# Attention over a long context: probabilities transposed on VectorE and moved by SBUF transfers instead of on TensorE, blocks handled in pairs

## The reference

```python
Q_char = _linear(layernorm(x), Wq_c, bq_c)                 # 256 x 512
K_sub  = _linear(ctx, Wk_s, bk_s)                          # 25088 x 512
V_sub  = _linear(ctx, Wv_s, bv_s)
scores = einsum('bqh,bkh->bqk', Q_char, K_sub) / sqrt(512)
char2sub = einsum('bqk,bkh->bqh', softmax(scores), V_sub)
...
x = x + gate * char2sub + (1 - gate) * sub2char            # sub2char: the other direction, on sampled rows
x = x + attention(layernorm(x)); x = x + moe(layernorm(x))
```

## Time and profile before

| | us |
|---|---|
| median of 3 runs (lowest, highest) | 1259.25 (1258.22, 1261.04) |
| profiled execution, its own time | 1258.86 |
| its span, first to last instruction | 1257.0 |
| prologue, to the first matmul of the block loop | 78.6 |
| block loop, to the last addition of `acc` | 654.0 |
| one block in the loop | 11.77 |
| busy in the span: PE, DVE, ACT | 1117.1, 578.9, 392.4 |

### The profile page before, as it was taken

The page is one execution under the profiler, slowest core; times in us unless marked ns, Lnnn a source line. Parts: engine busy times, 40 slices in busy tenths (PEclk is TensorE's granted clock), DMA queues, the critical chain, the costliest instruction groups (busy, mean ns, idle before and its releaser), DMA issues.

```text
span 1257.0 us, 17677 instructions
## 1 busy us (share of the span) xinstructions
PE 1117.1 (89%) x7048; PEld 785.6 (62%) x7048; DVE 578.9 (46%) x955; ACT 392.4 (31%) x645; POOL 3.5 (0%) x20
## 2 busy tenths in 40 slices
PE   9999999999999999999999989998876656665767
PEld 8768888888888888888887657655322222222223
DVE  2367777777777777777743165220110010001001
ACT  1254554554554554554522163101100000000000
POOL 1000000000000000000000000000000000000000
PEclk9999999999999999999999989999998998989988
DMA  9158455455455455455508315997999999999996
GB/s 361 69 224 331 153 194 188 154 192 190 153 191 191 151 191 192 151 190 193 174 1 351 118 67 202 373 380 290 422 418 421 421 425 421 422 422 421 423 419 283
DMA packets 84780, 331.07 MB, mean 263 GB/s; under 512 B 3600, under 2 KB 3728, under 8 KB 75408
## 3 DMA queue, kind: packets, MB, share of 16 engines
q1 hardware_dynamic: 84752, 330.66, 67.7%
HBM read 330.12 MB, written 0.52 MB: 263 GB/s over the span
## 4 chain that ended last, share of the span: by engine, by line
PE 71%; SPq 23%; DMA 3%; DVE 2%; issue 1%; ACT 1%; DVEq 0%
SPq L372 17%; PE ps L507 7%; PE ps L508 7%; PE ps L528 7%; PE ps L509 7%; PE ps L530 7%; PE ps L529 7%; SPq L374 4%; PE ps L516 3%; DMA wu<-in_r_up 2%; SPq L376 2%; PE ps L764 2%; PE ps L482 2%; PE ps L495 2%; PE ps L832 2%; PE ps L802 1%
## 5 line engine op out<-in xcount | busy, mean ns | idle before, releaser
L507 PE MATMUL ps<-ctt_hi,q_hi 128*128 128x512 f32 x392 | 156.9, 400 | 0.9 <-DVE gate L1182 0.9
L508 PE MATMUL ps<-ctt_lo,q_hi 128*128 128x512 f32 x392 | 152.8, 390 | 0.0
L509 PE MATMUL ps<-ctt_hi,q_lo 128*128 128x512 f32 x392 | 152.7, 390 | 0.0
L530 PE MATMUL ps<-nat_hi,pt_lo 128*128 128x512 f32 x392 | 152.7, 389 | 0.0
L528 PE MATMUL ps<-nat_hi,pt_hi 128*128 128x512 f32 x392 | 152.6, 389 | 0.1
L529 PE MATMUL ps<-nat_lo,pt_hi 128*128 128x512 f32 x392 | 152.5, 389 | 0.0
L1347 DVE TENSOR_TENSOR hh<-sg,ps 128x256 f32<-128x256 f32 x32 | 13.5, 421 | 263.0 <-PE ps L808 263.0
L1092 DVE TENSOR_TENSOR nat_lo<-nat,nat_hi 128x2048 fp32r<-128x2048 f32 x49 | 112.3, 2292 | 24.5 <-ACT nat_hi L892 24.5
L832 PE MATMUL ps<-wd,hh_t 128*32 128x512 f32 x512 | 76.9, 727 | 42.3 <-DMA wd<-in_r_down 39.5
L1087 DVE TENSOR_TENSOR ctt_lo<-ctt,ctt_hi 128x2048 fp32r<-128x2048 f32 x49 | 111.9, 2284 | 0.0
L902 ACT ACTIVATE pexp<-ps,st 128x512 f32<-128x512 f32 x98 | 66.6, 686 | 138.6 <-DVE st L1108 138.6
(11 more groups left out here) (252 smaller groups left out, 1367.7 us busy)
## 6 DMA issues: line engine op xcount, KB each, us to landing
wu<-in_r_up SPq DMA_DIRECT2D x32, 2048.0 KB, 30.3
wd<-in_r_down SPq DMA_DIRECT2D x32, 2048.0 KB, 34.0
wg<-in_r_gate SPq DMA_DIRECT2D x31, 2048.0 KB, 36.4
ctt<-in_ctx_t SPq DMA_DIRECT2D x49, 1024.0 KB, 5.1
nat<-in_ctx_rows SPq DMA_DIRECT2D x49, 1024.0 KB, 7.4
w_gate<-in_w_g_t SPq DMA_DIRECT2D x2, 1024.0 KB, 11.5
w_k<-in_w_k SPq DMA_DIRECT2D x1, 2048.0 KB, 13.5
w_v<-in_w_v SPq DMA_DIRECT2D x1, 2048.0 KB, 11.7
```

Source lines behind the costliest of these rows:

```text
L507: mm(o, qh, ctt_hi[par][:, c, :], start=(c == 0), stop=False)
L508: mm(o, qh, ctt_lo[par][:, c, :], start=False, stop=False)
L509: last = mm(o, ql, ctt_hi[par][:, c, :], start=False, stop=(c == HC - 1))
L530: last = mm(o, pt_lo[:, q, t, :], nat_hi[par][:, t, :], start=False, stop=(t == KT - 1))
```

## The change

Four things change together in the block loop:

1. The 8 TensorE transposes of a block are gone for 48 of the 49 blocks. VectorE transposes each 32x32 piece of `pexp` in place of them (`turn`, one instruction of 1024 elements per partition for each block, output `turned`), and then 16 DMAs from SBUF to SBUF (`spread`, 32 partitions with 2 KB each, once per pair) carry each 32-partition strip to the strip where it belongs, in `pt`. `probs_hi` and `probs_lo` read `pt` from SBUF.
2. Blocks are handled in pairs (24 pairs, and block 48 by itself with TensorE transposes). The scores of a pair take four PSUM banks; there is one `pair_bias` and one `alpha` per pair, and the products of both blocks of a pair are accumulated in PSUM before one `accumulate`.
3. `ctt_lo` now lies on top of `ctt`, and `nat_lo` on top of `nat`. So a buffer of `ctt` is free for the next load only when its `scores` are done, and one of `nat` when its `products` are done. SP waits for these.
4. `scores(1)` is moved ahead of the loop in place of 32 small filling matmuls; 46 filling matmuls behind the loop go.

```diff
+            def spread(u):
+                sp.wait_ge(s["turned_ready"], u * 2 + 2)
+                for g in range(G):
+                    for k in range(G):
+                        sp.dma_start(pt[k * Q:(k + 1) * Q, g, :, :, :], turned[g * Q:(g + 1) * Q, k, :, :, :]
+                                     ).then_inc(s["pt_loaded"], 16)
+            def pair(u, last=False):                      # SP
+                sp.wait_ge(s["scores_ready"], u * 2 + 1)
+                load_columns(u * 2 + 2, 0)
+                sp.wait_ge(s["scores_ready"], u * 2 + 2)
...
+                    load_columns(u * 2 + 3, 1)
+                sp.wait_ge(s["products_done"], u * 2 - 1)
+                load_rows(u * 2, nat[0], nat_loaded[0])
+                spread(u)
+                sp.wait_ge(s["products_done"], u * 2)
+                load_rows(u * 2 + 1, nat[1], nat_loaded[1])
...
+            with pe.Fori(1, NS) as u:                     # TensorE
+                for half in range(2):
+                    scores(u * 2 + half, half)
+                for half in range(2):
+                    pair_product(u - 1, half)
-                    scores(b, par)
-                    products(b - 1, 1 - par)
-                    transpose_probs(b)
...
+            def pair(u, par, last=False):                 # ScalarE
+                rows_hi(u - 1, 0)
+                probs_hi(u - 1, 0)
+                rows_hi(u - 1, 1)
+                probs_hi(u - 1, 1)
+                columns_hi(u * 2 + 2, 0, u * 16 + 32)
+                exps(u, par)
+                if not last:
+                    columns_hi(u * 2 + 3, 1, u * 16 + 32)
...
+            def turn(b, half):                            # VectorE
+                dve.wait_ge(s["exp_ready"], b + 1)
+                dve.transpose(turned[:, :, half, :, :], pexp[:, half, :, :].rearrange("p w (k j) -> p k w j", k=G)
+                              ).then_inc(s["turned_ready"], 1)
+            def pair(u, par, sums=True, last=False):
+                if sums:
+                    accumulate(u - 2, par)
+                rows_lo(u * 2 - 2, nat[0], nat_hi[0], nat_lo[0])
+                block_max(u * 2, 0)
+                probs_lo(u * 2 - 2, 0)
+                rows_lo(u * 2 - 1, nat[1], nat_hi[1], nat_lo[1])
+                probs_lo(u * 2 - 1, 1)
+                step(block_max(u * 2 + 1, 1))
+                pair_bias(par)
+                columns_lo(u * 2 + 2, 0)
+                for half in range(2):
+                    turn(u * 2 + half, half)
+                if not last:
+                    columns_lo(u * 2 + 3, 1)
```

More of the change, by code:

```diff
@@ L22 @@
 NB = NK // BLK
+NS = NB // 2
+Q = 32
+G = P // Q
 KT = BLK // P
@@ L334, in _ @@
                 sp.dma_start(flat(dst), runs(a[src])).then_inc(s["watt_loaded"], 16)
[L335 to L340, removed]
+            with sp.Fori(4, NS - 1) as u:
+                pair(u)
+            pair(NS - 1, last=True)
+            sp.wait_ge(s["scores_ready"], NB)
@@ new lines, in exps @@
+            def exps(u, par, halves=2):
+                act.wait_ge(s["bias_ready"], u + 1)
+                for half in range(halves):
+                    for q in range(QT):
+                        last = act.activation(pexp[:, half, q * KT:(q + 1) * KT, :].rearrange("p t n -> p (t n)"),
+                                              ps[:, 2 * half + q, :], ACT.Exp, bias=nbias[:, q:q + 1],
+                                              accum_out=rsum[par][:, 2 * half + q:2 * half + q + 1])
+                    last.then_inc(s["exp_ready"], 1)
+                act.activation(alpha[par], dmax, ACT.Exp).then_inc(s["alpha_ready"], 1)
@@ L1196, in _ @@
-            with dve.Fori(0, (NB - 1) // 2 - 1) as i:
-                step.enter(i, 8)
-                two_blocks(i)
-            step.leave((NB - 1) // 2 - 1)
-            two_blocks((NB - 1) // 2 - 1, last=True)
-            probs_lo(NB - 1)
-            accumulate(NB - 1, 0)
+            pair(1, 1, sums=False)
+            with dve.Fori(1, NS // 2 - 1) as i:
+                step.enter(i - 1, 12)
+                pair(i * 2, 0)
+                pair(i * 2 + 1, 1)
+            step.leave(NS // 2 - 2)
@@ new lines, in _ @@
+            pair(NS - 2, 0)
+            pair(NS - 1, 1, last=True)
+            accumulate(NS - 2, 0)
+            rows_lo(NB - 3, nat[0], nat_hi[0], nat_lo[0])
+            step(block_max(NB - 1, 0))
+            pair_bias(0, halves=1)
+            probs_lo(NB - 3, 0)
+            rows_lo(NB - 2, nat[1], nat_hi[1], nat_lo[1])
+            probs_lo(NB - 2, 1)
+            rows_lo(NB - 1, end_nat, end_nat_hi, end_nat_lo)
+            dve.wait_ge(s["pt_hi_ready"], NB)
+            dve.tensor_tensor(end_pt_lo[:, :, :].rearrange("p (q t) n -> p q (t n)", q=QT), bank(4, 2),
+                              end_pt_hi[:, :, :].rearrange("p (q t) n -> p q (t n)", q=QT).bitcast(F32),
+                              ALU.subtract).then_inc(s["pt_lo_ready"], 1)
```

261 lines of the change are left out of this document (141 added, 120 removed).

## The result

| | us |
|---|---|
| before, median of 4 runs (lowest, highest) | 1258.74 (1255.91, 1261.04) |
| after, median of 4 runs | 1355.84 (1355.19, 1357.19) |
| after / before, 95% interval | 1.0776 [1.0758, 1.0794] |
| profiled execution after: time, span | 1355.61, 1353.8 |

The kernel is 97 us slower. The sign was predicted; 1287 was 69 us too low, and 1356 lies outside the range of 1256 to 1335.

A forecast was written before the change was run, and what follows sets the result against it. TensorE bounds the loop before; after, a queue circle of 24.84 us per pair was to. Start 98.5, 22 laps 546.5, weight loads 6 and tail 30.9 end the loop at 681.9, 27.9 later: 1287 us, range 1256 to 1335.

The forecast's parts named there:

- The circle: Block loop, from one pair's second turn through strips, `nat` load, VectorE's work to the next second turn: 24.84 us per pair.
- sixteen issues: SP's queue in each pair: sixteen SBUF transfers issued 0.44 us apart, 7.04 us of the lap.
- "0.37" and "0.57": Bounds per strip issue on SP: shortest duration of one issue, and distance of two loop issues with an address computed between.
- under 5.8 us or over 9: Sign for SP's sixteen issues in the loop: the prediction is wrong if they take less or more than this.
- the turn: VectorE's 32x32 transpose of 1024 elements, taken as the one-input copy's 1.22 us, two per lap 2.44.
- the three with a weight load: Three loop laps with a 2 MB weight issued between `nat` and the next `ctt`: 2.0 us more each, 6 together.
- The end of the loop moves the kernel one for one: Expert loads start when the product after the loop is done, so a later loop end, 27.9 us, delays the kernel equally.
- 3.0 us: TensorE's room per pair, 24.84 - 21.8, before matmuls slowed by a falling clock in its gaps would show.
- Rivals 1, 2 and 4: Issue cheaper than any row, 1238 us, chance 0.08; TensorE stays the bound, 1211, 0.08; no difference, 1259, 0.06.
- Rival 3: VectorE's turn takes two passes, 2.28 us each, 1334 us; or slow strips delay `nat`, 1338; chance 0.15.
- second rival: TensorE stays the bound, strips costing their bytes instead of issues: lap 20.7, below 21.8, time 1211 us; chance 0.08.
- TensorE 21.8: TensorE's matmuls in one pair of the loop without transposes: four runs of 24 matmuls, 4 x 5.45 = 21.8 us.

The follow-up runs named there:

- rows_late: Kernel after, ScalarE and VectorE reordered so that what waits for the second `nat` stands behind what the next turn needs; 1233.72 us, ratio 0.9795.
- split_act: Kernel after with eight of the sixteen strips issued by ScalarE's queue, the other eight by SP; 1251.08 us, ratio 0.9940.
- rows_first: Kernel after with the load of the pair's second `nat` issued on SP ahead of the strips; 1346.96 us, ratio 1.0694.
- late_split_192: Kernel after with the edits of `rows_late` and `split_act`, and `st` padded to put stationary operands at 224 of 256 bytes; 1219.20 us, ratio 0.9691.
- after_pad: Kernel after with `st` padded so the stationary operands lie at 96 of 256 bytes; 1354.72 us, ratio 1.0756, 0.233 us per matmul.
- hbm_strips: Kernel after with the sixteen transfers reading from HBM instead of SBUF, so values differ; 1434.3 us in a single run, end of loop 685.1.

## Why the prediction was right in sign and wrong in size

**What bounds the loop.** Right, and shown. The circle that begins with "VectorE's second `turn` of a pair releases the sixteen SBUF transfers" sets the lap, with no matmul in it: `rows_late` took `nat` out of it and the lap went from 27.4 to 22.4, `split_act` halved its issues and it went to 22.7, and with HBM as source it was 24.77 to the 24.84 worked out.

**The step that failed** is the term "sixteen issues ... I take 0.44, between the two: 7.04", and its bounds "0.37" and "0.57". It measured 0.63, or 10.02 us. The prediction itself said that "None in the trace is from SBUF to SBUF or over 32 partitions", and then took the price and both bounds from issues with HBM at one end. The upper bound was the distance of two issues with an address between them, which is no bound on an unseen kind of transfer. The 22 laps have 22 x (10.02 - 7.04) = 66 us more of it and the tail 2.9, of the 69 by which the loop ended later than predicted. That this one term makes up the whole is in part luck: the other terms of the lap came out 0.25 us shorter together, 5 us in 22 laps, and the start, the weight loads and the rest of the tail about as much longer. "I am wrong if SP's sixteen take under 5.8 us or over 9": they took 10.02.

**The terms beside it.** Each of the others of the lap came within 0.25 us; the turn is 1.2 us as read from the copy. The loop ends 751.2 instead of 681.9: 2.2 at its start (second turn at 100.7, not 98.5), 22 laps 614.9 instead of 552.5, tail 35.5 instead of 30.9. In the 22 laps the three with a weight load are 2.7 us longer than the others each (30.3 against 27.58), where 2.0 was allowed. Of the tail's 4.6, 2.9 are once more the sixteen issues (725.76 - 715.71 = 10.05), about 0.8 the last block's transposes, which the sum had left out (737.33 to 738.12), and about 0.5 the last 48 matmuls, 11.4 us from 738.12 to the last sum in place of 10.9. The tail was also added up 0.15 too high: its terms make 30.75, not 30.9.

**The end of the loop moves the kernel one for one.** Right: 97.2 and 97.

**The clock.** That slower matmuls would first use up the room beside the circle held in the kernel after: the clock fell, a pair's products took 2 us more, and the lap was still the sum of the circle's terms. The room was 27.4 - 22.4 = 5.0 us, not the "3.0 us" of the prediction, as the circle was longer. `rows_first` is the case where the clock shows.

**The signs.** The issues "under 5.8 us or over 9" is the sign that came. Two others were read wrong: VectorE's longest wait was expected to be `nat_lo`, ScalarE's the one for `nat`, and both were those for the strips (108.9 against 89.4 us, 219.6 against 75.2), which lie beside the circle. The longest wait of an engine is not the proof of a bound; taking an edge out, as `rows_late` does, is.

**The rivals.** Rivals 1, 2 and 4 need an issue cheaper than 0.44; it was dearer. Rival 3's times, 1334 and 1338, came nearer than the forecast, but by mechanisms that did not happen: a turn took 1.2 us, as the copy of its size, and not 2.28, and a strip landed 2.0 us after its issue, `nat` in 5.4. The second rival's 1211 is what the change offers once the circle is open: `late_split_192` is 1219. The Trainium skill's sentence behind it ("DMA: Bandwidth & Descriptors", Issuing engines are not separate DMA queues), that the time on the sequencer is "usually small relative to the DMA itself", is not this trace's case: one issue took 0.63 us of a queue where the transfer landed 2.0 us after its issue, and sixteen took 10.0. What the same section of the Trainium skill says of several issuing engines, that they save only that time, agrees with `split_act`: 5.05 us less of issues, 4.7 less in the lap.

**"TensorE 21.8."** The term held only for operands in the old place. The change also moved `q_hi` from 224 to 32 of 256, and with that its TensorE bound was 22.4; this lay below the circle's 27.4. That it costs the kernel after next to nothing is argued from that: `after_pad` could not show it, as its padding did not bring the pace back, and no run has the kernel after at 224.

## What to carry to other kernels

When work leaves an engine for DMA transfers, count the issues on the queue before the bytes, and if no row shows a transfer with the same two ends, measure one by itself instead of bounding it by transfers of another kind. Follow the released transfer through everything that is queued behind it on each engine: the 42 us that leave TensorE are real, but come only when no circle of queues is longer than TensorE's part, and opening one circle can show another just behind it. When a change moves buffers, compare the distance of two matmuls before and after, since the place of an operand alone was worth 1.1% here.

## What the runs showed of the hardware that was not expected

- An issue on SP takes 0.63 us when source and destination are both in SBUF, whether it moves 32, 64 or 256 KB and over 32 or 128 partitions; 0.457 us from HBM for the same 64 KB, and 0.47 to HBM (two issues only). Eight issues on SP take 4.97 us while ScalarE issues eight of its own in 5.31 us; so SP takes as long for each as without them (0.62 and 0.63). What ScalarE would take alone no run shows. Why both ends in SBUF cost more stays open.
- 64 bytes in the place of the stationary operands (f32r, SBUF) change the distance of matmuls of 128x512 from 0.227 to 0.233 us, with a granted clock of 1.00 in both. Byte 224 of 256, where the streamed `ctt_hi` lies too, was fast, 32 and 96 were slow. Whether the rule is in the difference of the two places or in one of them stays open; no other place was tried. In the kernel after `pt_lo` lay at 224 and `pt_hi` at 32, and the pace of the products was 0.233.
- After idle gaps of 3.2 to 3.4 us per pair TensorE's matmuls came every 0.43 us for a while, about half the pace, and the granted clock was 0.79 from 455 to 461. In `hbm_strips`, with 1.95 us idle in 28, it was 1.00 (the row of its window, columns as in the earlier trace rows) and 0.99 from 100 to 600:

```profile
412.00:440.00 28.00, 26.05 (x111) 20.16 (x109) 19.61 (x22) 13.27 (x16) 0.00 (x0) 1.00 0.60 210
```
